# Attention's far exponentials: a square on VectorE and GpSimd in place of ScalarE, with key tiles in a mixed order

## The chip, the core and the metric

The kernel runs on one core of a Trainium2 chip. Times are microseconds of one execution on the device. The engines are TensorE (PE, its weight loads PEld), VectorE (DVE), ScalarE (ACT), GpSimd (POOL) and SyncE (SP), which issues most of the DMAs. Each works through its own queue in order, and semaphores order the queues among each other.

## The reference

Two sequences of 2048 tokens with 256 channels pass a layer norm, an attention with 16 heads of 16 channels, and a feed-forward part with shared and routed experts. What matters here is the attention (S = 2048):

```python
scores = jnp.einsum('bhqd,bhkd->bhqk', qh, k_rec) / math.sqrt(d)
t = jnp.arange(s, dtype=jnp.float32)
decay = jnp.exp(-LAMBDA_DECAY * jnp.abs(t[:, None] - t[None, :]))
scores = scores * decay[None, None, :, :]
attn = jax.nn.softmax(scores, axis=-1)
out = jnp.einsum('bhqk,bhkd->bhqd', attn, v_rec)
```

With LAMBDA_DECAY = 0.01, a score between tokens over 1024 rows apart is multiplied by less than exp(-10.24).

## The kernel before

It has three stages: a prologue (layer norm, values, first keys and queries), the attention, and the feed-forward part. The attention goes through 2 x 16 = 32 heads, numbered n = 2 it + par, in 16 pairs. `pairs` (line 505) writes the first and the last pair out and runs the others in two loops of one pair a round.

A head is 16 key tiles of 128 keys (step s), each against all 2048 queries in two halves of 1024. For each half PE makes scores into two banks of PSUM (`scores`, line 675). Three such pairs of banks take turns (`half_of`, line 482). The decay is put into keys and queries beforehand, so that only the tile's own block on the diagonal needs a correction: DVE multiplies it in PSUM with a mask (`mask`, line 591). ACT takes the exponential of the half, PSUM to SBUF (line 760), into one of three buffers of probabilities (`probs_of`, line 491). No maximum is subtracted, and the sums of the softmax come from a column of ones among the values. PE multiplies the probabilities with the values, four chunks of 512 queries side by side (`products`, line 685), and sums over the 16 tiles in a bank of its own for odd and one for even heads.

The queues are written out by hand:

- PE takes for step s: scores of half 0, products of step s - 2, scores of half 1 (lines 707 to 715); after step 4 the four transposes of the head in front (line 693), and in even heads of the first 12 pairs a projection for a later unit of heads after step 7 and one after step 11 (`project`, line 669).
- DVE takes the mask of each step, after step 2 a copy of the sums of the head in front (line 615), after step 5 their normalisation (line 619), and in even heads of the first 12 pairs three pieces after steps 8, 9 and 10 and three after steps 12, 13 and 14, which turn a projection into new keys or queries (`prepare`, lines 596 to 613, called in lines 646 to 649).
- ACT takes two exponentials a step.
- POOL copies the next head's values (line 562) when the products of the head in front are done, and in even heads of the first 12 pairs, before that, the weights of the next projection (line 565).
- SP stores prepared keys and queries and loads those of the next head (`load_halves`, line 146: 16 DMAs a head), from the time that the scores of the head in front are done.

Scores of a half wait until ACT has emptied the banks, three halves back. Both rings of three start anew with a head or a pair of heads, while 16 and 32 are no multiples of 3; so at the beginning of a head waits are for one half or one tile less far back:

```python
def halves_done(n, s, half):
    h = 2 * s + half
    return n * NHALF + (h - 1 if h < 2 else h - 2)
def tiles_done(par, n, s):
    return n * NSTEP + (s - 1 if par == 0 and s < 2 else s - 2)
```

ACT waits with `tiles_done` for the products that read the buffer of probabilities before (line 758).

Of the kernel before, what the change touches and what calls it, by code (L numbers as in the profile page):

```python
# [15 lines left out]
P = 128  # L16
# [415 lines left out]
def attention(nc, sem, ident, xT, V_all, decay, small, w_qk, w_unit, K_st, Q_st, work, ps, attn_dram, halves_dram, first_block, late_keys, **_):  # L432
# [17 lines left out]
    names = ("vg w proj_ps proj_free prep_link prep_sb sc_ps masked exp_done pv_done o_sb oT_ps rden_sb att_sb").split()  # L450
    s_ = {n: sem("a_" + n) for n in names}
    s_.update(att_out=sem("a_att_out"), stk0=sem("a_stk0"), stk1=sem("a_stk1"), out0=sem("a_out0"), out1=sem("a_out1"))
    bd_all, bd_link, flag = sem("a_bd_all"), sem("a_bd_link"), sem("a_flag")
# [28 lines left out]
    def half_of(s, half):  # L482

        return 2 * ((2 * s + half) % (ACC // 2))

    def halves_done(n, s, half):

        h = 2 * s + half
        return n * NHALF + (h - 1 if h < 2 else h - 2)

    def probs_of(par, s):

        return (par * NSTEP + s) % 3

    def tiles_done(par, n, s):

        return n * NSTEP + (s - 1 if par == 0 and s < 2 else s - 2)

    def own_block(s):

        at = s * P % HALF
        bank = half_of(s, s * P // HALF) + at // CH
        return ps[:, bank, at % CH:at % CH + P]

    def pairs(eng, pair):
        pair(0, True, True, False)
        with eng.Fori(1, NPAIR - PPU) as it:
            pair(it, True, False, False)
        with eng.Fori(NPAIR - PPU, NPAIR - 1) as it:
            pair(it, False, False, False)  # L510
        pair(NPAIR - 1, False, False, True)

    with nc.Block() as block:
        @block.sync
        def _(sp):
# [5 lines left out]
            def pair(it, prep, first, last):  # L521
# [35 lines left out]
        def _(pool):  # L557
            first_block["gpsimd_start"](pool)
            prime(pool, "vg", "w", "att_out", "stk0", "stk1", "out0", "out1")
# [9 lines left out]
            def pair(it, prep, first, last):  # L569
# [17 lines left out]
        def _(dve):  # L587
            first_block["vector_start"](dve)
            prime(dve, *"proj_free prep_link prep_sb masked o_sb rden_sb att_sb".split())

            def mask(n, s):

                wait(dve, "sc_ps", n * NHALF + 2 * s + s * P // HALF + 1)
                nc.vector.tensor_tensor(own_block(s), own_block(s), dmask, ALU.mult).then_inc(s_["masked"], 1)  # L594
# [41 lines left out]
            def pair(it, prep, first, last):  # L636
# [28 lines left out]
        def _(pe):  # L665
# [9 lines left out]
            def scores(par, n, s, half):  # L675
                wait(pe, "exp_done", halves_done(n, s, half))
                for q0, w, a in score_pieces(s, half):
# [3 lines left out]
                    m = nc.tensor.matmul(ps[:, half_of(s, half) + c % 2, q0 % CH:q0 % CH + w],  # L681
                                         K_st[tile, par, a, s * P:(s + 1) * P], Q_st[tile, par, a, at:at + w], start=True, stop=True)
                m.then_inc(s_["sc_ps"], 1)

            def products(par, n, s):

                wait(pe, "exp_done", n * NHALF + 2 * s + 2)
                for c in range(QC):
                    m = nc.tensor.matmul(ps[STRIP * c:STRIP * (c + 1), ACC + par], Vg[:, par, s], probs[:, probs_of(par, s), chunk(c)],  # L689
# [9 lines left out]
            def pair(it, prep, first, last):  # L699
                for par in range(2):  # L700
                    n = it * 2 + par
                    idle = ACC + 1 - par
# [1795 lines left out]
```

## Time and profile before

| what | us |
|---|---|
| runs, median of 3 (lowest, highest) | 1466.76 (1463.68, 1467.51) |
| span of the profiled execution (no other time of it is given) | 1469.9 |
| busy in it: PE, PEld | 1318.5, 587.3 |
| busy in it: ACT, DVE, POOL | 1145.2, 545.4, 214.7 |

The span runs from the first to the last instruction of one execution. Busy time of PE is that of matmuls, whose ends are modelled; PEld are weight loads beside them. In the rows further down, L760 is line 760 of the kernel, `ps` stands for PSUM, `work` for the large buffer in SBUF that holds probabilities, values and more.

### The profile page before, as it was taken

How to read it: one execution, taken by the hardware profiler on the slowest of the kernel's cores; microseconds unless marked ns; L12 is line 12 of the kernel's file. 1: busy time of each engine (PE TensorE's matmuls, PEld its weight loads, DVE VectorE, ACT ScalarE, POOL GpSimd, SP SyncE). 2: the span in 40 equal slices, each digit the busy share in tenths (PEclk: the TensorE clock that was granted, in tenths of full speed). 3: DMA queues.
4: the chain of work that ended last, by engine and by line, in shares of the span. 5: the costliest groups of instructions: out<-in, count | busy, mean ns of one | idle time of the engine just before them, and what ended most of it. 6: DMA issues, size and time to landing. Idle time of an engine off the chain costs nothing. (4 is left out here: it accounts for less than half of the span.)

```text
span 1469.9 us, 26673 instructions
## 1 busy us (share of the span) xinstructions
PE 1318.5 (90%) x8496; PEld 587.3 (40%) x8497; DVE 545.4 (37%) x1700; ACT 1145.2 (78%) x1419; POOL 214.7 (15%) x249
## 2 busy tenths in 40 slices
PE   7969999999999999999999999999987877879881
PEld 4623333333333333333333333333335655666641
DVE  4612323132232323323232222112223657674754
ACT  4559899998999999899999999999972444544531
POOL 2410000000000000000000000000002453333574
PEclk9979999999999999999999999999997997899996
DMA  7775566655466655556664555544973224457843
GB/s 190 233 181 146 127 153 153 133 143 120 117 158 138 156 111 143 121 139 155 139 152 93 143 121 127 111 93 100 239 150 85 82 95 154 149 183 215 266 131 101
DMA packets 141091, 210.96 MB, mean 144 GB/s; under 512 B 56864, under 2 KB 102816, under 8 KB 132768
## 3 DMA queue, kind: packets, MB, share of 16 engines
q1 hardware_dynamic: 134496, 192.86, 53.1%
q0 software_dynamic: 6144, 16.79, 3.6%
q8 instruction: 30, 0.49, 0.2%
q10 hardware_dynamic: 384, 0.52, 0.1%
q14 instruction: 37, 0.30, 0.1%
HBM read 147.19 MB, written 67.11 MB: 146 GB/s over the span
## 5 line engine op out<-in xcount | busy, mean ns | idle before, releaser
L760 ACT ACTIVATE work<-ps 128x1024 f32<-128x1024 f32 x1024 | 951.6, 1089 | 70.1 <-DVE ps L594 36.9
L689 PE MATMUL ps<-work 128*32 128x512 f32 x4096 | 548.5, 608 | 0.0
L681 PE MATMUL ps<-Q_st,K_st 64*128 64x512 f32 (+3 forms) x2432 | 440.9, 429 | 43.4 <-ACT work L760 28.3
L681 PEld LDWEIGHTS ps<-Q_st,K_st 64*128 64x128 f32 x2432 | 231.0, 184 | 541.9 <-ACT work L760 450.2
L594 DVE TENSOR_TENSOR ps<-ps,small 128x128 f32<-128x128 f32 x512 | 153.2, 299 | 728.9 <-PE ps L681 727.5
L562 POOL COPY work<-V_all 128x256 f32 (+1 forms) x32 | 12.8, 401 | 924.7 <-PE ps L689 924.0
L689 PEld LDWEIGHTS ps<-work 128*32 128x32 f32 x4096 | 80.9, 108 | 113.8 <-issue 87.8
L2120 POOL DMA_INDIRECT xs_dram<-part,decay x64 | 67.3, 1051 | 56.2 <-DVE decay L1888 24.0
L2138 POOL DMA_INDIRECT xT<-y_dram,decay x64 | 65.2, 1019 | 62.9 <-DMA xT<-y_dram,decay 31.2
L2297 PE MATMUL ps<-stack,work 128*128 x384 | 54.5, 288 | 0.2 <-issue 0.2
L2297 PEld LDWEIGHTS ps<-stack,work 128*128 128x128 f32 x384 | 50.2, 204 | 1.1 <-issue 1.1
L671 PE MATMUL ps<-xT,w_unit 128*128 (+1 forms) x96 | 47.6, 618 | 0.0
L2267 PE MATMUL ps<-decay,work 128*128 128x256 f32 x128 | 34.8, 427 | 11.7 <-DVE work L2346 11.7
L2204 ACT ACTIVATE work<-work,small 128x256 f32<-128x256 f32 x32 | 16.9, 590 | 35.1 <-POOL small L2146 35.0
L2353 DVE COPY work<-ps 128x512 f32<-128x512 f32 x48 | 33.0, 688 | 24.7 <-PE ps L2279 20.6
L2191 ACT COPY small<-stack 64x256 f32 x48 | 19.3, 402 | 29.1 <-PE ps L2316 24.2
L2279 PE MATMUL ps<-ident,work 128*128 128x128 f32 x192 | 32.4, 294 | 9.9 <-DVE work L2353 8.1
L2182 ACT ACTIVATE decay<-ps 128x128 f32<-128x128 f32 x48 | 13.2, 275 | 35.2 <-PE ps L2297 28.3
L2315 PE MATMUL ps<-stack,work 64*128 x96 | 34.9, 445 | 5.7 <-ACT work L2196 2.9
L2249 PE MATMUL ps<-xT,w_qk 128*128 128x512 f32 x64 | 32.7, 635 | 5.5 <-DVE work L2346 4.5
L1713 PE MATMUL ps<-w_qk,work 128*128 128x256 f32 x128 | 35.0, 433 | 2.7 <-ACT work L1747 2.7
L2196 ACT COPY work<-ps 128x512 f32<-128x512 f32 x48 | 28.1, 585 | 11.7 <-DMA y_dram<-work 5.4
(181 smaller groups left out, 1047.9 us busy)
## 6 DMA issues: line engine op xcount, KB each, us to landing
K_st<-halves_dram SPq DMA_DIRECT2D x248, 256.0 KB, 5.6
halves_dram<-work SPq DMA_DIRECT2D x64, 512.0 KB, 3.7
Q_st<-halves_dram SPq DMA_DIRECT2D x248, 128.0 KB, 5.6
work<-xs_dram SPq DMA_DIRECT2D x96, 128.0 KB
y_dram<-work SPq DMA_DIRECT2D x48, 256.0 KB
work<-in_L_attn_x SPq DMA_DIRECT2D x16, 512.0 KB, 4.8
attn_dram<-work SPq DMA_DIRECT2D x16, 256.0 KB, 6.6
work<-attn_dram SPq DMA_DIRECT2D x8, 512.0 KB
```

The source lines that it names most:

```text
L594: nc.vector.tensor_tensor(own_block(s), own_block(s), dmask, ALU.mult).then_inc(s_["masked"], 1)
L671: m = nc.tensor.matmul(ps[:, bank], w_unit[:, which, k], xT[:, k, at:at + CH] if isinstance(at, int) else xT[:, k, bass.ds(at, CH)], start ...
L681: m = nc.tensor.matmul(ps[:, half_of(s, half) + c % 2, q0 % CH:q0 % CH + w], K_st[tile, par, a, s * P:(s + 1) * P], Q_st[tile, par, a, at: ...
L689: m = nc.tensor.matmul(ps[STRIP * c:STRIP * (c + 1), ACC + par], Vg[:, par, s], probs[:, probs_of(par, s), chunk(c)], start=s == 0, stop=s ...
L760: nc.scalar.activation(probs[:, probs_of(par, s), half * HALF:(half + 1) * HALF], src, ACT.Exp, scale=SCALE).then_inc(s_["exp_done"], 1)
L1713: m = nc.tensor.matmul(bank[:, j * D:(j + 1) * D], aT[:, k, at:at + P], w_o[:, k], start=k == 0, stop=k == KD - 1)
L2120: nc.gpsimd.indirect_dma_start(xs_dram[r // 4], bass.IndirectOffsetOnAxis(ap=at, axis=0), xn[r % 2][:, j], None).then_inc(put_done[r % 2][ ...
L2138: nc.gpsimd.indirect_dma_start(yg[n % 2][:, j, i], None, y_dram[b], bass.IndirectOffsetOnAxis(ap=at, axis=0)).then_inc(fetched(n, j, i), 16)
L2267: m = nc.tensor.matmul(ps[:, down_banks(r)[half], j * D:(j + 1) * D], hid_s[:, h, at:at + P], w_ds[:, h], start=h == 0, stop=h == NSH - 1)
L2297: m = nc.tensor.matmul(ps[:, GU[g % 2], at:at + P], xsT[:, g % 2, k, a], w_gu[:, k * NE * P:(k + 1) * NE * P][:, bass.ds(experts[i][a], P) ...
L2315: nc.tensor.matmul(ps[:, DOWN[0], 0:D], hT[0:MR, g % 2], w_dr[0:MR, bass.ds(experts[i][0] * 2, D)], start=True, stop=True)
L2353: nc.vector.tensor_copy(xsT[:, g % 2].rearrange("p k a t -> p (k a t)"), ps[:, TR]).then_inc(tr_sb, 1)
```

## The change

The score of a key tile against a chunk of 512 queries, all of them over 1024 rows away, is so small that 1 + x + x²/2 stands for its exponential. There is one such chunk for the key tiles 0 to 3 (the last chunk) and 12 to 15 (the first chunk): 8 of 16 tiles, the far ones. For these DVE reads the chunk from PSUM and writes 1 + x, POOL squares it in place and then takes half of it plus a half. ACT does only the other chunk of that half, 512 columns in place of 1024. The half with the far chunk comes first in a far tile, that with the own block first in a near one. From the second head on, tiles come in an order in which near and far ones alternate. The very last head leaves all on ACT. PSUM banks and buffers of probabilities are numbered through all heads, for which the loop now takes three pairs a round: three rounds, then five pairs written out. POOL's copy of weights moves from the beginning of an even head to its step 2.

```diff
+    MIXED = [4, 0, 5, 1, 6, 2, 7, 3, 8, 12, 9, 13, 10, 14, 11, 15]
+    FAR_CHUNK = {kt: QC - 1 if kt < KT // 4 else 0 for kt in NATURAL if kt < KT // 4 or kt >= KT - KT // 4}
+    def half_of(turn, s, k):
+        return 2 * ((turn * NHALF + 2 * s + k) % (ACC // 2))
+    def halves_done(n, s, k):
+        return n * NHALF + 2 * s + k - 2
+    def probs_of(turn, s):
+        return (turn * NSTEP + s) % RING
+    def tiles_done(n, s):
+        return n * NSTEP + s - 2
     def pairs(eng, pair):
-        pair(0, True, True, False)
-        with eng.Fori(1, NPAIR - PPU) as it:
-            pair(it, True, False, False)
-        with eng.Fori(NPAIR - PPU, NPAIR - 1) as it:
-            pair(it, False, False, False)
-        pair(NPAIR - 1, False, False, True)
+        pair(0, True, True, False, 0)
+        with eng.Fori(1, 1 + 3 * RING, RING) as it:
+            for j in range(RING):
+                pair(it + j, True, False, False, (1 + j) % RING)
+        for it in range(1 + 3 * RING, NPAIR - 1):
+            pair(it, it < NPAIR - PPU, False, False, it % RING)
+        pair(NPAIR - 1, False, False, True, (NPAIR - 1) % RING)
...
+            def far_probs(turn, n, s, order):
+                kt = order[s]
+                if kt not in FAR_CHUNK:
+                    return
+                done = n * NFAR + far_before(order, s) + 1
+                p = probs[:, probs_of(turn, s), chunk(FAR_CHUNK[kt])]
+                wait(pool, "far_read", done)
+                nc.gpsimd.tensor_tensor(p, p, p, ALU.mult).then_inc(s_["far_sq"], 1)
+                wait(pool, "far_sq", done)
+                pool.sem_inc(far_link, 1)
+                nc.gpsimd.tensor_scalar(p, p, 0.5, 0.5, ALU.mult, ALU.add).then_inc(s_["far_sb"], 1)
...
-                    if par == 0 and prep:
-                        wait(pool, "proj_ps", 2 * it)
-                        weights((it // PPU + 1) % KD)
                     if not (last and par):
                         wait(pool, "pv_done", n * NSTEP)
                         values(n + 1, 1 - par)
+                        for s in range(NSTEP):
+                            if s == 2 and par == 0 and prep:
+                                wait(pool, "proj_ps", 2 * it)
+                                weights((it // PPU + 1) % KD)
+                            far_probs(turn, n, s, order)
...
+            def read_far(first, turn, n, s, kt):
+                c = FAR_CHUNK[kt]
+                wait(dve, "sc_ps", n * NHALF + 2 * s + 1)
+                if not (first and tiles_done(n, s) <= 0):
+                    wait(dve, "pv_done", tiles_done(n, s))
+                nc.vector.tensor_scalar(probs[:, probs_of(turn, s), chunk(c)], ps[:, half_of(turn, s, 0) + c % 2], SCALE, 1.0,
+                                        ALU.mult, ALU.add).then_inc(s_["far_read"], 1)
...
-                    for s in range(NSTEP):
-                        mask(n, s)
+                    for s, kt in enumerate(NATURAL if first and par == 0 else MIXED):
+                        if kt in FAR_CHUNK and not (last and par):
+                            read_far(first, 2 * third + par, n, s, kt)
+                        mask(2 * third + par, n, s, kt)
...
+            def scores(first, turn, n, s, k, order, far):
...
+                if not (first and halves_done(n, s, k) <= 0):
+                    wait(pe, "exp_done", halves_done(n, s, k))
+                if far or 2 * s + k < 3:
+                    far_read(first, n, s, k, order)
...
+            def products(turn, n, s, order, far):
...
                 wait(pe, "exp_done", n * NHALF + 2 * s + 2)
+                if far and kt in FAR_CHUNK:
+                    wait(pe, "far_sb", n * NFAR + far_before(order, s) + 1)
...
+                            chunks = [c for c in (2 * half, 2 * half + 1) if (last and par) or c != FAR_CHUNK.get(kt)]
+                            bank = half_of(turn, s, k) + chunks[0] % 2
+                            src = ps[:, bank:bank + len(chunks)].rearrange("p a b -> p (a b)")
+                            nc.scalar.activation(probs[:, probs_of(turn, s), chunks[0] * CH:(chunks[-1] + 1) * CH], src, ACT.Exp,
                                                  scale=SCALE).then_inc(s_["exp_done"], 1)
```

`far_read` on PE waits, three halves on, until DVE has read a far chunk.

## Rows read from the trace of the kernel before

**Rows 1.** Busy time by stage: stretch, us, PE, PEld, DVE, ACT, POOL, clock, DMA, GB/s.
```profile
86.20:1101.00 1014.80, 982.30 (x6774) 345.04 (x6774) 284.95 (x776) 956.24 (x1034) 21.60 (x46) 0.99 0.60 137
1101.00:1469.90 368.90, 275.77 (x1484) 197.70 (x1476) 219.25 (x797) 153.21 (x302) 161.22 (x167) 0.87 0.47 146
```

**Rows 2.** The same for heads 13, 14 (with projections) and 24.
```profile
500.96:531.30 30.34, 29.52 (x218) 10.29 (x212) 5.96 (x19) 29.58 (x32) 1.02 (x2) 1.00 0.58 133
531.30:564.37 33.07, 32.25 (x212) 11.27 (x216) 13.43 (x31) 29.91 (x33) 0.40 (x1) 1.00 0.60 139
848.34:877.83 29.49, 28.67 (x204) 10.01 (x208) 5.96 (x19) 29.48 (x33) 0.40 (x1) 1.00 0.55 111
```

**Rows 3.** Timeline of ACT in head 13: start, length, then what.
```profile
510.20 20.41 ACT L760 ACTIVATE work<-ps 128x1024 f32<-128x1024 f32 x22
```

**Rows 4.** Waits of the whole execution: us in total, times, longest.
```profile
ACT work L760 <- PE ps L689: 10.6, 15, 0.8
```

**Rows 5.** Timeline of PE in head 13.
```profile
507.22 1.07 PE L689 MATMUL ps<-work 128*32 128x512 f32 x8
...
508.65 0.66 PE L696 MATMUL ps<-ident,work 128*128 128x128 f32 x4
...
509.72 1.06 PE L689 MATMUL ps<-work 128*32 128x512 f32 x8
...
511.37 1.06 PE L689 MATMUL ps<-work 128*32 128x512 f32 x8
...
514.69 1.06 PE L689 MATMUL ps<-work 128*32 128x512 f32 x8
...
516.42 1.06 PE L689 MATMUL ps<-work 128*32 128x512 f32 x8
...
518.26 1.06 PE L689 MATMUL ps<-work 128*32 128x512 f32 x8
```

**Rows 6.** Timeline of PE in head 14, around the first projection.
```profile
544.21 0.50 PE L681 MATMUL ps<-Q_st,K_st 64*128 64x512 f32 x2
...
546.56 0.50 PE L681 MATMUL ps<-Q_st,K_st 64*128 64x512 f32 x2
546.98 1.07 PE L689 MATMUL ps<-work 128*32 128x512 f32 x8
547.98 0.50 PE L681 MATMUL ps<-Q_st,K_st 64*128 64x512 f32 x2
```

**Rows 7.** Timeline of ACT beside it: in brackets the idle time before.
```profile
547.09 1.02 ACT L760 ACTIVATE work<-ps 128x1024 f32<-128x1024 f32 x1 [0.98 <-PE ps L681]
548.85 6.52 ACT L760 ACTIVATE work<-ps 128x1024 f32<-128x1024 f32 x7 [0.74 <-DVE ps L594]
```

**Rows 8.** Groups of ACT by shape: busy us, mean ns, idle before.
```profile
L2169 ACT ACTIVATE work<-ps 128x512 f32<-128x512 f32 x16 | 9.5, 594 | 18.3 <-PE ps L2249 18.3
```

**Rows 9.** Timeline of DVE in head 14, after the first projection.
```profile
548.52 0.30 DVE L594 TENSOR_TENSOR ps<-ps,small 128x128 f32<-128x128 f32 x1 [4.89 <-PE ps L681]
...
550.44 0.68 DVE L607 TENSOR_REDUCE small<-ps 128x1 f32<-128x512 f32 x1
...
551.23 0.69 DVE L610 CAST work<-work 128x1024 fp32r<-128x1024 f32 x1
...
552.11 1.21 DVE L613 TENSOR_TENSOR work<-work 128x1024 fp32r<-128x1024 f32 x1
```

**Rows 10.** Groups of DVE by shape.
```profile
L617 DVE COPY work<-ps 128x512 f32<-128x512 f32 x32 | 21.8, 680 | 9.2 <-PE ps L689 9.2
```

**Rows 11.** Groups of POOL by shape.
```profile
L265 POOL TENSOR_TENSOR work<-work 128x1024 fp32r<-128x1024 f32 x8 | 18.8, 2354 | 27.3 <-DVE work L303 27.3
...
L565 POOL COPY w_unit<-w_qk 128x512 f32 x11 | 6.7, 614 | 1.4 <-issue 0.2
...
L271 POOL TENSOR_TENSOR small<-small 128x4 f32<-128x4 f32 x8 | 1.6, 199 | 0.6
```

**Rows 12.** SP's DMA issues in head 13: the last of the next head's loads.
```profile
511.55 0.53 SPq L157 DMA_DIRECT2D Q_st<-halves_dram  x1
```

More of the change, by code:

```diff
@@ L519, in store_att, with pair @@
                 sp.dma_start(dst[bass.ds(it // (H // 2), 1), bass.ds(it % (H // 2), 1)].rearrange("b u p t d -> p (b u t) d"), att).then_inc(s_["att_out"], 16)
-            def pair(it, prep, first, last):
+            def pair(it, prep, first, last, third):
                 for par in range(2):
@@ L567, in _, with pair @@
             values(0, 0)
-            def pair(it, prep, first, last):
+            def far_probs(turn, n, s, order):
[9 more added lines that the diff above has]
+                nc.gpsimd.tensor_scalar(p, p, 0.5, 0.5, ALU.mult, ALU.add).then_inc(s_["far_sb"], 1)
+            def pair(it, prep, first, last, third):
                 for par in range(2):
                     n = it * 2 + par
-                    if par == 0 and prep:
-                        wait(pool, "proj_ps", 2 * it)
-                        weights((it // PPU + 1) % KD)
+                    turn = 2 * third + par
+                    order = NATURAL if first and par == 0 else MIXED
                     if not (last and par):
@@ L634, in set_flag, with pair @@
                 nc.vector.tensor_scalar(flags[:, 0:1], bound_new[:, 0:1], SAFE, None, ALU.is_gt).then_inc(flag, 1)
-            def pair(it, prep, first, last):
+            def pair(it, prep, first, last, third):
                 for par in range(2):
@@ L673, in project, with far_read @@
                 m.then_inc(s_["proj_ps"], 1)
-            def scores(par, n, s, half):
-                wait(pe, "exp_done", halves_done(n, s, half))
-                for q0, w, a in score_pieces(s, half):
+            def far_read(first, n, s, k, order):
+                g = 2 * s + k - 3
+                if first and n == 0 and g < 0:
+                    return
+                before, at = (n, g // 2) if g >= 0 else (n - 1, NSTEP + g // 2)
+                tiles = order if g >= 0 else NATURAL if first and n == 1 else MIXED
+                if g % 2 == 0 and tiles[at] in FAR_CHUNK:
+                    wait(pe, "far_read", before * NFAR + far_before(tiles, at) + 1)
+            def scores(first, turn, n, s, k, order, far):
+                par = turn % 2
+                kt = order[s]
+                half = half_at(kt, k)
+                if not (first and halves_done(n, s, k) <= 0):
+                    wait(pe, "exp_done", halves_done(n, s, k))
+                if far or 2 * s + k < 3:
+                    far_read(first, n, s, k, order)
+                for q0, w, a in score_pieces(kt, half):
                     c = q0 // CH
@@ L697, in transposes, with pair @@
                 i.then_inc(s_["oT_ps"], 1)
-            def pair(it, prep, first, last):
+            def pair(it, prep, first, last, third):
                 for par in range(2):
                     n = it * 2 + par
+                    turn = 2 * third + par
                     idle = ACC + 1 - par
                     end = last and par
+                    order = NATURAL if first and par == 0 else MIXED
                     wait(pe, "vg", n + 1)
@@ L738, in _ @@
             for s in (NSTEP - 2, NSTEP - 1):
-                products(1, B * H - 1, s)
+                products((B * H - 1) % (2 * RING), B * H - 1, s, MIXED, False)
             first_block["router"](pe, 0, first_block["LG"])
```

76 lines of the change are left out of this document (40 added, 36 removed).

## The prediction

> **What bounds the kernel now.** I began with the stages: attention takes 1014.8 of the 1469.9 us of the profiled execution, and in it ACT is busy for 956 us and PE for 982 [rows 1]. Everything that the change touches lies there. The page has no separate time for this execution; its span lies 3.1 us over the median of the three runs shown (1466.76), so I sum differences and take them off that median.
>
> A busy PE says little, since ends of matmuls are modelled, so I looked next at single heads [rows 2]. Three lengths repeat: 30.34 us for an odd head, 33.07 for an even one with projections, 29.49 for an even one without. The 32 heads are 15 odd ones, 11 and 4 even ones of the two kinds, the first and the last. ACT in a stretch without stalls runs 22 exponentials in 20.41 us [rows 3]: less 1.1 for the last one, (20.41 - 1.1) / 21 = 0.92 us apart, or 1.84 for a tile of two, 29.4 for a head. That is the plain even head: **ACT bounds it**. The odd head has 0.9 more, at its end; 0.7 of it is ACT's wait for a product, 15 times, 10.6 us in all [rows 4]: the early wait of line 497.
>
> Then PE alone [rows 5]. After the transposes it has fallen behind, and from 509.72 to 514.69 its products come three tiles in 4.97 us, 1.66 each, with scores and products end to end; once it has caught up they come 1.84 apart (516.42, 518.26), at ACT's pace. So **PE needs 1.66 of ACT's 1.84 us**: it is the next limit, 10% behind. Of the 1.66, products take 1.00 (546.98 to 547.98 [rows 6]) and each half of scores 0.33. The transposes add 2.50 - 1.66 = 0.84. A projection puts the next scores 2.35 us behind those in front (544.21 to 546.56 [rows 6]) in place of 0.33, 2.0 more, and ACT stands still for much of it [rows 7].
>
> **The change, part by part.**
> *ACT gets less.* In 8 of 16 tiles one exponential has 512 columns in place of 1024. An ACTIVATE of 512 from PSUM lasts 0.594 us [rows 8], one of 1024 behind an idle stretch 1.02 [rows 7]: 0.43 less, so 0.49 apart. ACT then needs 24 x 0.92 + 8 x 0.49 = 26.0 us a head, 3.4 less. Over 30 heads this would be 103 us; it isn't to be had, for PE needs 16 x 1.66 + 0.84 = 27.4.
>
> *PE does as much as before*, with two waits more: for the read (before scores reuse its buffer) and for the scaled chunk (before far products). Both stand in front of everything PE has left, so ACT runs dry behind them when they are late; where they have been met, they cost nothing. But with three score buffers PE can't run at 1.66. For a near and a far tile: from the near tile's first scores to the far tile's second ones PE takes 1.66 + 0.33 + 1.00 = 2.99; scores to mask 0.54, mask to exponential 0.33 [rows 6, 9]; then ACT does that one and the next tile's first (0.92 each) and its second (1.02, and 0.04 to hand over, an estimate), whose buffer PE needs. That is 6.76 for two rounds, 3.38 a pair of tiles, against 3.32 for PE and 3.25 for ACT. A head: 8 x 3.38 + 0.84 = 27.9.
>
> *VectorE gets 8 reads a head.* A PSUM read of 512 columns takes 0.68 us [rows 10]; beside 16 masks that is 10 us of 28. The far tile's mask stands behind the read, but it needs the later scores anyway. It hides behind ACT and PE (uncovered, 0.68 each), except beside the projections: there a read and piece 1 (550.44 to 551.92, 1.48 us [rows 9]) stand in front of the third step's mask, and piece 2 (1.21) in front of the fourth step's read. By the order of lines 640 to 649 the mask starts some 0.8 us after PE and ACT could have used it, and the read 1.3 after it could; the second projection's read belongs to the last far tile, which no projection covers. I take 0.6 us for each projection (0 if slack takes it up, 1.3 if none does).
>
> *GpSimd gets two operations for each read.* The square has two inputs: 2.354 us for 1024 columns, 0.199 for 4 [rows 11], so 0.19 + 512 x 2.11 ns = 1.27. The scaling has one input and no row. Its bounds are the copy of 512 (0.614) and the two-input price (1.27) [rows 11]; I take 0.65, since the copy is nearest, with as many bytes in and out. With 0.08 between them (an estimate) a far tile takes GpSimd 2.0 of every 3.38 us. It must be in time too: scores 0.53 [rows 6, 7], read 0.68, hand-over 0.05, the 2.0, and 0.05 make 3.31 us after the far tile's first scores, and PE wants it at 3.38 + 0.33 = 3.71. There are 0.4 us to spare, and one far tile in a head hasn't got them: the copy of line 562 waits for the last products of the head in front and delays the first square by 0.65. That costs 0.25 a head. What such sums leave out (the odd head's last 0.2 now) I take as 0.25 too. An odd or plain head: 27.9 + 0.5 = 28.4; with projections 28.4 + 4.0 + 1.2 = 33.6.
>
> The subtraction of 1024 columns takes GpSimd 2.35 us and VectorE 1.21 [rows 9, 11]. The Trainium skill, "GPSIMD Engine Reference", section 4.1, sends elementwise work to VectorE for such a factor, about two with two inputs, and calls one-input work roughly line-rate. By its first half this change would lose wherever GpSimd ends last; the trace agrees with the factor, yet here the work fits beside PE, and by its second half the scaling is as cheap as I take it.
>
> *Order and numbering.* Near and far alternate, so GpSimd has two tiles' time for each. The first head keeps the natural order: four far tiles in a row at 2.0 against 1.84, twice, about +1.5. Buffers numbered through remove the early wait, which the 28.4 already holds. Three loop rounds of three pairs and straight code in place of one-pair loops: nothing, as head 1 runs outside a loop now and is as long as the other odd ones (the wait of line 497 comes in both). The weights' copy (0.614 [rows 11]) now stands behind one far tile: two tiles' time covers it. The next head's loads are issued by 512.1 in a head that ends at 531.3 [rows 12]; one of 28 us still covers them.
>
> *Sum.* Odd: 15 x (28.4 - 30.34) = -29. Even with projections: 11 x (33.6 - 33.07) = +6. Plain even: 4 x (28.4 - 29.49) = -4. First +1.5, last (all on ACT) 0. Together -26: **1441 us**.
>
> **The rivals.**
> (a) *PE at its bare pace*: nothing lost at the buffers, at GpSimd or beside the projections. Heads of 27.4 and 31.4: 15 x 2.94 + 11 x 1.67 + 4 x 2.09 = 71 less, 1396. For it: 1.66 was held for three tiles [rows 5]. Against: there ACT was ahead, which it won't be.
> (b) *Slower: the scaling costs what two inputs cost*, 1.27. Then the far chunk comes 3.93 us after its scores, and each of the eight pairs of tiles is 0.22 longer: 28.4 + 1.8 = 30.2, and 34.8 with projections, which hide some. -2 + 19 + 3, and 3 for the first head: +23, 1490. The point is a price of 1.05, where the 3.71 us are used up. Against it the copy's 0.614; for it that no row shows GpSimd with two steps of arithmetic.
> (c) *GpSimd and VectorE hold each other up.* No row shows a two-input operation of GpSimd beside VectorE's piece 1 or 2, which would now lie together. If whichever starts first makes the other wait, the cast of 0.69 or the subtraction of 1.21 [rows 9] waits for up to 1.27, or holds up a square, with a mask or a read behind it. At 1 us for each of 22 projections, 1463. The Trainium skill, "SBUF — State Buffer", section "Who interferes with whom", has such a lock for VectorE's two-input operations and for its copies in a two-port mode. No run here shows it.
> That the change doesn't take the columns off ACT has nothing for it.
>
> **How the numbers follow.** The forecast has 0.47, (a) 0.13, (b) 0.19, (c) 0.15; 0.06 is left for what I don't see, half of it slower. 0.3% is 4.4 us, about what a measurement of this kernel can tell from no change. Faster: 0.47, 0.13, a third of (c) and a little of the rest, 0.67. Same: most of (c), 0.11. Slower: (b) and half of the rest, 0.22. The forecast's own range is 1420 to 1460 (0 to 1.3 us a projection, up to 0.9 for the scaling). For 8 in 10 it takes in (c), the near part of (a) and what lies short of (b): 1410 to 1478.
>
> **What would show it.** Products 1.69 apart on PE in heads without projections; ACT busy under 27 us of 28.4; short exponentials near 0.49 apart; squares near 1.27 and scalings near 0.65 us; scores released by ACT, products seldom by GpSimd. A scaling over 1.05 us with products waiting for GpSimd proves me wrong by (b); longer casts or subtractions on VectorE point to (c); even heads at 31.4 to (a).

## The result, and the profile after

The changed kernel takes **1455.36 us** (median of 4 runs, 1452.27 to 1457.08) against 1465.22 us (1463.22 to 1467.51) for the kernel before on the same chip: ratio 0.9919, interval [0.9898, 0.9941]. It is faster by 9 to 15 us, where 26 were forecast. The profiled execution took 1457.08 us and spans 1453.1; before, the span was 1469.9. Of the 16.8 us between the spans 3.1 lie ahead of attention, where nothing was changed (over all the profiles that stretch takes 83.1 to 86.2 us), 13.4 in attention, and 0.3 behind it.

The stages (first two rows, as in [rows 1]) and single heads (as in [rows 2]): stretch, us, busy PE, PEld, DVE, ACT, POOL, clock, DMA share, GB/s. The heads are 11, 10 and 24, then 7, 8 and the last one; the last row is the beginning of head 8.

```profile
83.08:1084.45 1001.37, 971.47 (x6774) 340.50 (x6776) 451.81 (x1025) 870.96 (x1034) 432.44 (x543) 0.99 0.61 140
1084.45:1453.10 368.65, 277.44 (x1484) 198.72 (x1476) 219.15 (x797) 153.19 (x302) 160.82 (x167) 0.87 0.47 146
433.68:462.35 28.67, 28.48 (x214) 10.00 (x210) 11.32 (x27) 26.81 (x34) 14.01 (x18) 1.00 0.60 139
400.36:433.68 33.32, 32.26 (x216) 11.12 (x216) 18.82 (x39) 27.15 (x33) 13.78 (x19) 1.00 0.61 142
838.38:866.78 28.40, 28.38 (x212) 9.99 (x208) 11.34 (x27) 26.77 (x33) 13.63 (x17) 1.00 0.60 122
305.22:336.17 30.95, 28.08 (x208) 9.98 (x208) 11.33 (x27) 26.91 (x34) 14.04 (x18) 1.00 0.60 144
336.17:371.69 35.52, 34.28 (x224) 11.43 (x216) 18.82 (x39) 27.27 (x33) 13.76 (x18) 0.95 0.51 122
1037.18:1080.69 43.51, 35.50 (x230) 14.12 (x226) 11.97 (x46) 34.68 (x42) 2.76 (x5) 0.96 0.62 143
336.10:340.30 4.20, 4.20 (x24) 1.01 (x17) 0.73 (x2) 2.54 (x3) 0.07 (x1) 0.59 1.03 220
```

The three ordinary kinds of head are what was forecast: 28.67 (28.4 forecast), 33.32 (33.6) and 28.40 (28.4). In the plain one ACT is busy for 26.77 of 28.40 us and bounds it no longer; PE is busy for 28.38, as far as its modelled ends tell. The rows that stand out are heads 7 and 8 (13 and 14 are like them, 30.99 and 35.36) and the last head, 43.51 in place of 39.66. Summed over heads, in us:

| heads | before | after | difference | forecast |
|---|---|---|---|---|
| odd, without 7 and 13 (13) | 394.7 | 371.9 | -22.8 | -25 |
| with projections, without 8 and 14 (9) | 297.5 | 299.6 | +2.1 | +5 |
| plain even (4) | 118.0 | 113.6 | -4.4 | -4 |
| first | 34.3 | 36.1 | +1.9 | +1.5 |
| 7, 8, 13, 14 | 126.8 | 132.8 | +6.0 | -3 |
| last | 39.7 | 43.5 | +3.9 | 0 |

The whole shortfall is in the last two lines: 9 us in the four heads, 4 in the last.

Groups by shape, as in [rows 10 and 11]: the square, the scaling and the read.

```profile
L604 POOL TENSOR_TENSOR work<-work 128x512 f32<-128x512 f32 x248 | 257.9, 1040 | 413.5 <-DVE work L646 413.5
L607 POOL TENSOR_SCALAR work<-work 128x512 f32<-128x512 f32 x248 | 154.3, 622 | 49.1 <-POOL work L604 49.1
L646 DVE TENSOR_SCALAR work<-ps 128x512 f32<-128x512 f32 x248 | 171.2, 690 | 286.5 <-PE ps L752 286.1
```

VectorE's subtraction beside a projection takes 1.21 us, as before [rows 9], in every head but the first: in those heads GpSimd's scaling has ended 0.73 us before the subtraction begins. In the first head, whose tiles keep the natural order, the second subtraction and a square lie together, and the subtraction takes 2.08 us:

```profile
115.34 1.04 POOL L604 TENSOR_TENSOR work<-work 128x512 f32<-128x512 f32 x1 [0.21 <-DVE work L646]
...
115.38 2.08 DVE L666 TENSOR_TENSOR work<-work 128x1024 fp32r<-128x1024 f32 x1
```

Waits of the whole execution. The line of [rows 4], exponentials waiting for products, is gone; products wait little for the scaled chunk; weight loads for scores stand behind ACT (450.2 us before), and exponentials behind the mask. The third row is new: PE's scores waiting for "issue", twice, up to 2.7 us at a time. "Issue" stands where the profile names nothing that the engine waited for.

```profile
PEld ps L752 <- ACT work L841: 259.9, 307, 1.7
ACT work L841 <- DVE ps L638: 109.2, 157, 2.2
PE ps L752 <- issue: 5.4, 2, 2.7
PE ps L764 <- POOL work L607: 3.6, 13, 0.9
```

Timeline, three places: the end of head 7, PE in head 24 (compare [rows 5]), and PE in the last head.

```profile
332.10 0.50 PE L752 MATMUL ps<-Q_st,K_st 64*128 64x512 f32 x3
...
335.30 0.50 PE L752 MATMUL ps<-Q_st,K_st 64*128 64x512 f32 x2 [2.70 <-issue]
...
335.83 0.30 DVE L638 TENSOR_TENSOR ps<-ps,small 128x128 f32<-128x128 f32 x1 [2.89 <-PE ps L752]
336.17 1.02 ACT L841 ACTIVATE work<-ps 128x1024 f32<-128x1024 f32 x1 [2.17 <-DVE ps L638]
...
337.17 1.22 PE L752 MATMUL ps<-Q_st,K_st 64*128 64x512 f32 x4
...
850.13 1.07 PE L764 MATMUL ps<-work 128*32 128x512 f32 x8
...
863.99 1.06 PE L764 MATMUL ps<-work 128*32 128x512 f32 x8
...
1052.38 0.63 PE L1789 MATMUL ps<-ident,work 128*128 128x128 f32 x4 [1.79 <-issue]
```

From 332.60 to 335.30 PE does nothing, and the profile names no buffer, signal or transfer that releases it. The queues of VectorE and ACT take up nothing for 2.8 and 2.9 us (from 332.79 and 333.10), though ACT still works on an exponential until 334.01. That is where the first round of the loop of line 533 ends: in all three queues the last record is the loop's branch. The second round ends at 523 us with the same picture. Behind it the granted clock is 0.59 for 4.2 us (last row of the heads' fence), its lower level of 1.2 GHz for most of them, and four matmuls of scores take 1.22 us together that take 0.73 elsewhere. In the last head PE stands for 1.79 us. Its queue is at line 1778, which waits for the loads of the next stage's constants, and the last of these lands at 1052.29. Again the lower level follows.

### The profile page after: what moved, and what is told of

It is laid out like the page before. It is cut to its first block and busy times, and to the rows that moved or that the text cites. A ratio compares the mean times of both kernels' runs of the same rounds, so it can differ in the third digit from the quotient of the medians.

```text
span 1453.1 us, 27412 instructions
## 1 busy us (share of the span) xinstructions
PE 1307.9 (90%) x8496; PEld 582.6 (40%) x8497; DVE 711.9 (49%) x1948; ACT 1059.6 (73%) x1419; POOL 624.5 (43%) x745
## 5 line engine op out<-in xcount | busy, mean ns | idle before, releaser
L841 ACT ACTIVATE work<-ps 128x1024 f32<-128x1024 f32 (+1 forms) x1024 | 866.0, 928 | 139.4 <-DVE ps L638 109.2
L752 PE MATMUL ps<-Q_st,K_st 64*128 64x512 f32 (+3 forms) x2432 | 422.8, 423 | 33.6 <-ACT work L841 14.3
L604 POOL TENSOR_TENSOR work<-work 128x512 f32<-128x512 f32 x248 | 257.9, 1040 | 413.5 <-DVE work L646 413.5
L752 PEld LDWEIGHTS ps<-Q_st,K_st 64*128 64x128 f32 x2432 | 225.0, 185 | 515.8 <-ACT work L841 259.9
L646 DVE TENSOR_SCALAR work<-ps 128x512 f32<-128x512 f32 x248 | 171.2, 690 | 286.5 <-PE ps L752 286.1
L607 POOL TENSOR_SCALAR work<-work 128x512 f32<-128x512 f32 x248 | 154.3, 622 | 49.1 <-POOL work L604 49.1
L2285 ACT ACTIVATE work<-work,small 128x256 f32<-128x256 f32 x32 | 16.9, 590 | 34.4 <-POOL small L2227 34.3
L2263 ACT ACTIVATE decay<-ps 128x128 f32<-128x128 f32 x48 | 13.2, 276 | 36.2 <-PE ps L2378 36.1
```

Source lines behind the costliest of these rows:

```text
L604: nc.gpsimd.tensor_tensor(p, p, p, ALU.mult).then_inc(s_["far_sq"], 1)
L607: nc.gpsimd.tensor_scalar(p, p, 0.5, 0.5, ALU.mult, ALU.add).then_inc(s_["far_sb"], 1)
L646: nc.vector.tensor_scalar(probs[:, probs_of(turn, s), chunk(c)], ps[:, half_of(turn, s, 0) + c % 2], SCALE, 1.0, ALU.mult, ALU.add).then_i ...
L752: m = nc.tensor.matmul(ps[:, half_of(turn, s, k) + c % 2, q0 % CH:q0 % CH + w], K_st[tile, par, a, kt * P:(kt + 1) * P], Q_st[tile, par, a ...
L841: nc.scalar.activation(probs[:, probs_of(turn, s), chunks[0] * CH:(chunks[-1] + 1) * CH], src, ACT.Exp, scale=SCALE).then_inc(s_["exp_done ...
```

## The experiments

Times are medians; each ratio is to the kernel before, run beside it on the same chip. That kernel took 1465.22 to 1470.53 us there, so between experiments ratios and heads are compared more safely than times. The experiments put three questions: what the loop costs, what the last head waits for, and what the two parts of the change are worth.

**The loop written out.**

```diff
-        with eng.Fori(1, 1 + 3 * RING, RING) as it:
-            for j in range(RING):
-                pair(it + j, True, False, False, (1 + j) % RING)
-        for it in range(1 + 3 * RING, NPAIR - 1):
+        for it in range(1, NPAIR - 1):
```

> The changed kernel with its fourteen middle pairs of heads written out in place of three loop rounds of three pairs; nothing else differs. Theory: the two ends of loop rounds cost it 8 to 9 us (in the trace 2.9 us without an instruction on PE, ACT and DVE, and 3.4 us of half TensorE clock behind it, over heads 7, 8, 13 and 14). Then heads 7 and 13 come to 28.7 us (30.95 and 30.99 in the changed kernel), heads 8 and 14 to 33.2 (35.52, 35.36), and the time falls from 1455 to about 1446. Rival: what stretches these four heads sits at their loads or projections and only happens to fall at the end of a round; then the four heads keep their lengths and the time stays within 2 us of 1455.

1439.4 us, ratio 0.9805 [0.9777, 0.9832]. Heads 7, 8 and the last:

```profile
305.19:333.87 28.68, 28.59 (x212) 9.98 (x208) 11.34 (x27) 26.81 (x33) 14.09 (x18) 1.00 0.59 136
333.87:367.03 33.16, 32.18 (x220) 11.23 (x216) 18.47 (x39) 27.17 (x34) 13.80 (x18) 1.00 0.62 146
1027.23:1067.68 40.45, 33.99 (x230) 13.80 (x226) 11.87 (x46) 34.38 (x42) 2.76 (x5) 1.00 0.63 154
```

The four heads lose 9.1 us, as the theory said, and the clock stays at 1.00. The time fell by more, 16 us between the two medians: the last head is 3.1 shorter, since the constants happened to come almost in time there (PE waited 0.22 us), and nine heads with projections lost 0.13 each. That makes 13.4 us of attention; the other 2 to 3 are not explained. Against the kernel before, attention is now 26.8 us shorter.

**The long round in the kernel before.**

```diff
-        with eng.Fori(1, NPAIR - PPU) as it:
-            pair(it, True, False, False)
-        with eng.Fori(NPAIR - PPU, NPAIR - 1) as it:
-            pair(it, False, False, False)
+        with eng.Fori(1, 10, 3) as it:
+            for j in range(3):
+                pair(it + j, True, False, False)
+        for it in range(10, NPAIR - 1):
+            pair(it, it < NPAIR - PPU, False, False)
```

> The kernel before with its loop in the changed kernel's shape: three rounds of three pairs and the rest written out; order, numbering and exponentials are those of before. Theory: a round of three pairs costs 2.9 us without an instruction at each of its two ends, whatever the pairs do, and half clock behind it; the heads at these places grow by 4 us together at each end, and the time goes up by 6 to 9 us over the kernel before (1465 to about 1472). Rival: the gap comes from the changed pairs themselves (their waits on both sides of the end); then heads 7, 8, 13 and 14 keep 30.3 and 33.1 us and the time stays within 2 us.

1475.84 us, ratio 1.0067 [1.0044, 1.0089]: 9.8 us slower, a little over the theory's 6 to 9. Heads 7, 8, 13 and 14 grew by 2.7, 1.0, 2.3 and 1.3. The timeline at the first end of a round:

```profile
336.15 0.50 PE L682 MATMUL ps<-Q_st,K_st 64*128 64x512 f32 x3
...
339.71 0.50 PE L682 MATMUL ps<-Q_st,K_st 64*128 64x512 f32 x2 [3.05 <-issue]
...
341.75 1.02 ACT L761 ACTIVATE work<-ps 128x1024 f32<-128x1024 f32 x1 [3.41 <-PE ps L690]
```

Nothing of the change is in this kernel but the shape of its loop, and the stop is there. VectorE went on after 0.3 us this time, which led to the next run.

**Rounds of two pairs.**

```diff
-        with eng.Fori(1, NPAIR - PPU) as it:
-            pair(it, True, False, False)
-        with eng.Fori(NPAIR - PPU, NPAIR - 1) as it:
-            pair(it, False, False, False)
+        with eng.Fori(1, 11, 2) as it:
+            for j in range(2):
+                pair(it + j, True, False, False)
+        for it in range(11, NPAIR - 1):
+            pair(it, it < NPAIR - PPU, False, False)
```

> The kernel before with five loop rounds of two pairs (the rest written out). Rows so far: at the end of a round an engine stands for 2 to 3 us where its round has 422 (VectorE), 482 (ACT) or over 1500 (PE) instructions, and for 0.4 at most where it has 313 (SP), 278 (VectorE), 221 (GpSimd) or 162 (ACT, one pair); PE's 502 of one pair cost 0.1 to 0.3. Theory: what counts is the length of the engine's own round; with two pairs PE has some 1000 and stands for 2.5 to 3 us, VectorE (186) under 0.4, and ACT (322) lies between the rows; four ends inside the loop, at 3.5 us each as in the run with rounds of three, make it 12 to 16 us slower than the kernel before. Rival: the standing comes with what a round of three pairs does (registers, addresses), and two pairs cost under 1 us an end: within 4 us of the kernel before.

1483.2 us, ratio 1.0111 [1.0081, 1.0141]: 14 us slower, within the theory's 12 to 16. ACT (322 instructions a round) went on within 0.3 us and VectorE (186) within 0.4; PE stopped at each of the four ends. PE's waits for issue, from 120 to 1030 us, and its timeline at the second end:

```profile
PE ps L682 <- issue: 12.2, 4, 3.4
...
406.16 0.79 PE L682 MATMUL ps<-Q_st,K_st 64*128 64x512 f32 x2 [3.20 <-issue]
```

So it is each engine's own round that counts. The counts of PE leave out matmuls, of which there are as many as weight loads; with them its rounds have 926 instructions for one pair (no stop), 1850 for two and over 2700 for three (both 2.7 to 3.4 us by the rows here). ACT's limit lies between 322 and 482, VectorE's between 278 and 422. On PE's queue the record of the branch itself lasts 3.3 to 3.8 us at these ends, but 0.2 us at the ends of one pair in the kernel before and 0.1 at the last end of a loop, where nothing is repeated.

What the engines stand for can be seen among the transfers, of which the profile has a kind called "instruction" (queue, packets, MB, share of the DMA engines). Four stretches: the kernel before from 205 to 820 us, with ten ends of rounds of one pair; then one stop each, of the changed kernel (332.6 to 335.3), of the kernel before with rounds of three (336.6 to 339.7) and with rounds of two (402.0 to 406.2):

```profile
q1 hardware_dynamic: 46071, 83.33, 58.1%
...
q8 instruction: 1, 0.02, 2.2%
q14 instruction: 2, 0.02, 1.9%
...
q8 instruction: 1, 0.02, 2.0%
q14 instruction: 1, 0.01, 1.0%
...
q8 instruction: 1, 0.02, 1.8%
```

Through ten short rounds not one instruction is loaded. Each stop of PE, in all eight ends of long rounds, has one load on q8, which begins 0.9 to 1.5 us after PE's branch and takes 0.9 to 1.3. On q14 there are as many loads as other engines stop: two (ACT and VectorE), one (ACT), none. So at the jump back these engines wait for instructions. Which queue serves which engine is concluded from these counts, and why PE stands for 1.7 us and more after its load has ended is not explained. In the written-out kernel 57 such loads fall between 205 and 820 us, and from 84 to 1030 us PE has no wait for issue at all: loading alone stops nothing, the jump back does.

**The constants one head earlier.** In the changed kernel:

```diff
+                    if last and not par:
+                        wait(sp, "att_out", 16 * H // 2)
...
+                        first_block["sync"](sp)
                     if par == 0 and not first:
                         store_att(it - 1)
                     if end:
-                        wait(sp, "att_out", 16 * H // 2)
...
-                        first_block["sync"](sp)
```

> The changed kernel, loop as it is, but the loads of the next stage's constants are issued one head earlier on SP: behind the loads of head 31, in front of the store of pair 14, in place of behind that store. Theory: in the changed kernel the last head is 43.5 us long because PE waits 1.79 us for these constants at its first router transposes and runs at half clock for 3.4 us behind that; with the constants there in time it comes to 40.4 us (its length in the written-out kernel, where the wait was 0.22), 3 us less, and the time from 1455 to about 1452. Rival: the last head is long because the order of its tiles puts the masks and the router's work badly together; then it stays at 43 to 44 us.

The loads now stand ahead of pair 14's store on SP, where they stood behind it. 1453.85 us, ratio 0.9908 [0.9875, 0.994], and the last head is 45.30 us long, not 40.4. By itself this fits the rival, but a timeline of DVE in that head shows a fault of the edit:

```profile
1051.12 0.42 DVE L680 TENSOR_TENSOR work<-ps,small 128x256 f32<-128x256 f32 x1 [2.93 <-DMA attn_dram<-work]
```

Two of the constants' issues took 15.2 us together, and the store had to wait for them; the normalisation waited for that store, and masks and scores behind it. One wait had been put in the place of another.

**The constants two heads earlier**, ahead of no store that is waited for:

```diff
                         load_halves(sp, K_st, Q_st, halves_dram, n + 1, 1 - par, s_[f"stk{1 - par}"])
+                    if isinstance(it, int) and it == NPAIR - 2 and par:
+                        wait(sp, "att_out", 16 * H // 2)
...
+                        first_block["sync"](sp)
```

> The changed kernel, loop as it is, with the constants' loads of the next stage issued on SP behind the loads of head 30, two heads earlier than in the changed kernel and ahead of no store that is waited for: when they were issued one head earlier they stood in front of pair 14's store, and VectorE waited 2.9 us for that store. Theory: the last head is long because the constants are late, so that it comes to 40.2 to 40.5 us (43.5 in the changed kernel), and the time falls by 3 us to about 1452. Rival: the last head of this kernel is long for another reason, as the one-head experiment could be read: then it stays over 42.

1451.94 us, ratio 0.9886 [0.9859, 0.9913]. The last head:

```profile
1039.77:1080.05 40.28, 34.22 (x230) 13.81 (x226) 11.85 (x46) 34.35 (x42) 2.75 (x5) 0.98 0.46 93
```

The theory's length; the time alone couldn't tell 3 us apart. Late constants make 3.2 of the 3.9 us, the remaining 0.6 is not explained.

**The numbering alone**, written out:

```diff
-    MIXED = [4, 0, 5, 1, 6, 2, 7, 3, 8, 12, 9, 13, 10, 14, 11, 15]
-    FAR_CHUNK = {kt: QC - 1 if kt < KT // 4 else 0 for kt in NATURAL if kt < KT // 4 or kt >= KT - KT // 4}
+    MIXED = NATURAL
+    FAR_CHUNK = {}
-        return FAR_CHUNK[kt] // 2 if kt in FAR_CHUNK else kt * P // HALF
+        return 0
```

> The changed kernel written out, natural order of the tiles, no far chunks: all sixteen tiles of a head go to the exponentials on ACT as before, so that only the numbering of the buffers is left of the change. Theory: it takes away the wait at the end of the odd heads, which come to 29.5 us like the plain even ones (30.34 before); 15 heads by 0.85 are 13 us: about 1452. The far chunks with their order are then worth what is left, about 6 us against the written-out kernel with them (1446). Rival: the wait at the end of odd heads only moves to another place, heads stay at 30.3 and the time at 1465; then all of the gain is the far chunks'.

1449.78 us, ratio 0.9889 [0.9867, 0.9911]: 16 us off, a little more than the 13 expected. Heads with projections, odd, plain:

```profile
521.38:554.49 33.11, 33.11 (x222) 11.52 (x218) 13.27 (x31) 29.97 (x33) 0.96 (x2) 1.00 0.61 142
554.49:583.68 29.19, 29.19 (x208) 10.10 (x208) 5.96 (x19) 29.19 (x33) 0.40 (x1) 1.00 0.58 137
862.25:891.62 29.37, 29.37 (x212) 10.18 (x208) 5.96 (x19) 29.37 (x34) 0.40 (x1) 1.00 0.51 109
```

ACT is busy for all of 29.19 and 29.37 us. The far chunks, with all that VectorE and GpSimd do for them, take off the 10 us that are left to 1439.4: 0.5 us of an odd head, 1.0 of a plain one, nothing of one with projections, and the first head is 2 us longer.

**GpSimd's arithmetic left out**, in the changed kernel:

```diff
-                nc.gpsimd.tensor_tensor(p, p, p, ALU.mult).then_inc(s_["far_sq"], 1)
-                wait(pool, "far_sq", done)
-                pool.sem_inc(far_link, 1)
-                nc.gpsimd.tensor_scalar(p, p, 0.5, 0.5, ALU.mult, ALU.add).then_inc(s_["far_sb"], 1)
+                pool.sem_inc(s_["far_sb"], 1)
```

> The changed kernel without GpSimd's square and scaling (GpSimd only passes the signal on, so that far probabilities are left as VectorE's 1 + x). Theory: GpSimd is in time nearly everywhere; odd and plain heads fall by 0.25 us at most from 28.6 and 28.4, which is the price taken for the one far tile of a head that hasn't got the time, and the heads with projections by no more than 0.5: 3 to 9 us in all. Rival: GpSimd's arithmetic (or a lock with VectorE) is what keeps the heads at 28.4 in place of PE's bare pace of 27.4; then heads fall by about 1 us each, and with projections by 2, some 40 us.

1441.07 us, ratio 0.9824 [0.9796, 0.9852]. Heads 10, 11 and 24:

```profile
397.65:430.46 32.81, 32.19 (x216) 11.09 (x216) 18.41 (x39) 27.16 (x34) 1.02 (x2) 1.00 0.62 145
430.46:459.01 28.55, 28.55 (x214) 10.06 (x210) 11.39 (x27) 26.80 (x34) 0.40 (x1) 1.00 0.60 139
833.22:861.60 28.38, 28.38 (x212) 9.99 (x208) 11.41 (x27) 26.77 (x34) 0.40 (x1) 1.00 0.60 122
```

By heads the theory holds: 0.1 us of an odd head, nothing of a plain one, 0.5 of one with projections, and 1.3 of the first. Attention is 9.3 us shorter, 2.4 of them in the last head, where GpSimd had no such work: PE's wait for the constants there was 0.85 us in place of 1.79. The time fell by 14, more than either account of the heads gives; the rest is not explained.

**Natural order with the far chunks**, written out; only `MIXED = NATURAL`.

> The written-out kernel with its far chunks made on VectorE and GpSimd, but with the tiles of every head in natural order: four far tiles in a row at either end of a head, in place of near and far in turn. Theory: GpSimd takes 1.04 + 0.20 + 0.62 = 1.86 us for a far tile, more than PE's 1.66, and has one tile's time for it in place of two: odd and plain heads 29.5 to 30.5 us, those with projections 34 to 36.5, and a time of 1475 to 1505, over the kernel before. Rival: GpSimd's queue is long enough ahead that the order does not matter: heads within 0.3 us of the alternating ones, and about 1439.

1531.71 us, ratio 1.0445 [1.0416, 1.0474]. The direction is the theory's, the size beyond its 1475 to 1505: plain heads 30.56, but odd ones up to 32.1 and those with projections 36.65; attention is 87 us longer than in the written-out kernel. By the profile's names products waited 25.7 us for GpSimd (0.3 in the same stretch of the written-out kernel), and 52.0 us, once a head, for ACT. These waits, and the second kind at the beginning of a head without projections:

```profile
ACT work L838 <- DVE ps L635: 169.2, 232, 3.1
PE ps L761 <- ACT work L838: 52.0, 30, 1.7
PE ps L761 <- POOL work L604: 25.7, 45, 0.9
...
937.58 0.62 POOL L604 TENSOR_SCALAR work<-work 128x512 f32<-128x512 f32 x1 [0.20 <-POOL work L601]
...
938.34 1.06 PE L761 MATMUL ps<-work 128*32 128x512 f32 x8 [1.73 <-ACT work L838]
```

That kind is GpSimd's too: all 30 of these waits end 0.15 us after one of its scalings, while the exponentials of that tile had been done for 2 us. GpSimd copies the next head's values only when the last products of the head in front are done, so its first square of a head comes late, and in a row of far tiles it can't catch up: the next products come 1.82 us apart, where PE alone needs 1.66. Exponentials wait longer for masks as well (86.8 us in the written-out kernel), and in 12 of the 24 projections a subtraction and a square lay together and the subtraction took 2.08 us. The order also puts the near tiles in a row, which ACT bounds; what that costs by itself no run shows.

**No masks**, written out; the masks' operation on VectorE is left out, and ACT waits for the scores.

> The written-out kernel without VectorE's masks: the exponentials wait for the scores alone (the multiplication of the diagonal blocks by the decay mask is left out). Theory: what holds a head at 28.4 to 28.7 us over PE's bare 27.4 is the round trip through three score buffers, in which the mask stands between scores and exponential; without it the loop is about 0.3 us shorter than the 3.38 reckoned for a pair of tiles and PE's own 3.32 decide: plain heads 27.4 to 27.7 (28.4 now), odd ones 27.4 to 27.8 (28.7), those with projections about 32.1 (33.2). Rival: PE's matmuls themselves take longer than the 1.66 us of a tile when ACT is never ahead; then the heads stay within 0.3 us of 28.4 and 28.7.

1417.2 us in one run. Heads with projections, odd, plain:

```profile
510.54:542.51 31.97, 31.89 (x220) 10.88 (x216) 15.30 (x23) 27.16 (x33) 13.40 (x18) 1.00 0.62 140
542.51:570.95 28.44, 27.76 (x212) 9.46 (x208) 6.91 (x11) 26.70 (x34) 14.43 (x19) 1.00 0.62 149
840.46:868.26 27.80, 27.72 (x212) 9.45 (x208) 6.91 (x11) 26.72 (x34) 13.63 (x18) 1.00 0.52 115
```

Between the two: plain heads lose 0.6 us, a little short of the theory, those with projections 1.2, as it said, odd ones only 0.24, within the rival's bound. The mask is a limit in plain heads, by its place between scores and exponential or by VectorE's time for it, which this run doesn't separate; what holds the odd ones is open.

**VectorE's pieces in four steps**, written out:

```diff
                     nc.vector.tensor_tensor(bound[:, which:which + 1], bound[:, which:which + 1], bound_new[:, which:which + 1], ALU.max)
+                elif piece == 2:
                     nc.vector.tensor_copy(pt[:, :, 0].bitcast(F32R), split).then_inc(s_["prep_link"], 1)
-                elif piece == 2:
+                elif piece == 3:
-                        if prep and par == 0 and s >= 8 and s < 11:
+                        if prep and par == 0 and s >= 8 and s < 12:
-                        if prep and par == 0 and s >= 12 and s < 15:
+                        if prep and par == 0 and s >= 12 and s < 16:
```

> The written-out kernel with VectorE's work on a projection spread over four steps in place of three: the reduction and the running bound in the second, the cast in the third, the subtraction in the fourth. Theory: the second piece (1.48 us), which stands in front of the third step's mask, costs a projection about 0.4 us and the subtraction less; heads with projections fall from 33.16 to 32.3 to 32.8, eleven times, and the time from 1439 to about 1433. Rival: VectorE is early enough there and the projection's own matmuls on PE are all of the 4.5 us that these heads are longer; then they stay at 33.1.

**1429.53 us**, ratio 0.9743 [0.9709, 0.9777]: the lowest of the kernels that leave nothing out. A head with projections and the odd one behind it:

```profile
513.73:546.39 32.66, 32.46 (x222) 11.36 (x220) 18.56 (x39) 27.31 (x34) 15.45 (x18) 1.00 0.61 137
546.39:574.67 28.28, 28.28 (x208) 9.74 (x208) 11.35 (x27) 26.73 (x32) 13.86 (x18) 1.00 0.62 150
```

0.5 us less for the one, as expected, and 0.4 for the other, which was not. The subtraction now lies beside GpSimd's scaling, which takes 1.36 us in place of 0.62, 22 times; here the subtraction runs from 292.13 to 293.35:

```profile
292.47 1.36 POOL L604 TENSOR_SCALAR work<-work 128x512 f32<-128x512 f32 x1 [0.20 <-POOL work L601]
```

**This with the earlier constants**, at both places.

> Written out, constants one head earlier, and VectorE's pieces in four steps together. Theory: the parts add up, since they lie in different heads: 1439 less 6 for the pieces, and for the constants between 0 and 1 (the written-out kernel waited only 0.22 us for them): about 1433, under both kernels. Rival: the earlier constants' transfers hold up the keys and queries of head 31 or shorter heads uncover a transfer; then it is no better than the written-out kernel with the pieces in four steps.

> Written out, VectorE's pieces in four steps, and the constants' loads behind those of head 30. Theory: heads as in the run with the pieces in four (28.3 odd, 32.7 with projections, 28.4 plain) and a last head of 40.2 in place of 41.2: about 1428.5 against 1429.5, at any rate not slower. Rival: the constants' transfers in head 29 delay the loads of head 31, and head 31 starts late: slower than 1429.5 by 2 us or more.

One head earlier: 1434.09 us, 0.9771 [0.9735, 0.9807], last head 43.87: pair 14's store again, so the parts did not add up. Two heads earlier: 1432.71 us, 0.9756 [0.9735, 0.9778], last head 40.51 but head 30 0.7 longer. Neither can be told from the kernel without the earlier constants.

## Why the prediction was right or wrong

- **The bound and the sum by heads: right, in part by luck.** ACT's 29.4 us no longer bound a head: 28.67, 33.32 and 28.40 came, against 28.4, 33.6 and 28.4. Once the loop is out of the way, attention is 26.8 us shorter where the sum said 26, and the time is 1439.4 where it said 1441. But its parts are off and cancel: odd heads lost 26 us in all where 29 were forecast, those with projections grew by 1 in place of 6. Within a head too: from 850.13 to 863.99 eight products are 1.73 apart, where 1.69 was forecast, and a plain head has nothing of the 0.25 for GpSimd.
- **The loop: the step that failed.** "Three loop rounds of three pairs and straight code in place of one-pair loops: nothing, as head 1 runs outside a loop now". Head 1 could show that a round of one pair costs nothing (no engine stood over 0.33 us at its end), but not what a round of three costs. In the changed kernel three engines stand for 2.7 to 2.9 us at each end, and with the lower clock behind it an end costs 4.6 us, 9.1 for the two. That is shown from both sides: taken away by writing the loop out, added to the kernel before by its long round. What the engines stand for are loads of instructions at the jump back, seen among the transfers of all eight such ends. A rule of the Trainium skill, "Runtime: NRT & Kernel Launch", section "Instruction fetch mechanics", bears on it: an engine's memory holds 512 instructions, PE's 2048, and a taken branch to a place outside the current window of two pages must wait until that is fetched. The runs agree in kind, PE going on at 926 instructions where ACT stops at 482. By 512 and 2048 alone ACT, VectorE (422) and PE at 1850 would have had room for a whole round; they stop all the same, and the measurement decides.
- **The last head: failed too.** "last (all on ACT) 0" looked at its work and not at what it waits for. From the issue of the first of its loads to the landing of the last constant 32.1 us pass (31.3 before, 30.5 written out); PE asks for them 29.4 us after that issue (31.7 before, 29.4 written out), as the two heads over which they are loaded became shorter. The late constants cost 3.2 us, by the run with the constants two heads earlier.
- **GpSimd: right in effect, the square mis-sized.** 1.04 us where 1.27 was forecast, from a row of two different inputs; the scaling 0.62 where 0.65 was. Rival (b) had its point at 1.05 for the scaling and falls. The quarter of a us a head that was taken for GpSimd's lateness is 0.1 in odd heads, nothing in plain ones. That the order is needed is shown: natural order loses 92 us to the written-out kernel.
- **Rival (c): the lock is there, and the changed kernel misses it by luck.** The prediction knew no run that shows it and feared that VectorE's pieces and GpSimd's operations "would now lie together". In the changed kernel the subtraction lies beside none of them, in every head but the first: it begins 0.73 us after a scaling's end, a distance that no sum foresaw. Where they lie together, one holds up the other: the subtraction takes 2.08 us beside a square in place of 1.21, the scaling 1.36 beside a subtraction in place of 0.62. The cast kept its 0.68 in all these runs. Even so the kernel with 22 such scalings has the lowest time. **Rival (a)**: heads of 27.4 were not reached even without masks.
- **The projections**: 5.2 us over a plain head were forecast, 4.0 for PE and 1.2 for VectorE's pieces; 4.9 came. Splitting the pieces gave back 0.5, and 0.4 of the next head. GpSimd's arithmetic holds 0.5 of such a head, where the sum had the 0.25 of every head. How the rest is divided no run shows.

## What to carry to other kernels

When a change makes a loop's round longer, count the instructions of each engine's round and price the ends of rounds, with the clock behind them; in the rows the signs are a wait for "issue" of some us at the branch and a load of instructions in it. When heads or stages become shorter, look at every transfer whose cover was their length. And an operation taken off the bounding engine is worth only the distance to the next one: a plain head freed ACT of 2.6 us (29.37 to 26.77) and became 1.0 shorter, and over all heads 10 us came back.

## What the runs showed that was not expected

- A stop of 2.7 to 3.4 us of PE at the end of a round of 1850 instructions or more, none at 926; of ACT at 482 and VectorE at 422, none at 322 or fewer. In each stop instructions are loaded, and after each stop of PE the granted clock was at the 1.2 GHz level for 3.4 us or more.
- VectorE's subtraction of two inputs in SBUF and GpSimd's square or scaling hold each other up when they lie together: 2.08 us in place of 1.21, 1.36 in place of 0.62.
- GpSimd's square of a chunk with itself, 128 x 512, takes 1.04 us; its scaling with two steps of arithmetic takes 0.62, as long as a copy of that size [rows 11].
- An issue on SP can be what takes time: two DMAs into `w_unit` held SP for 12 to 15 us, and what stands behind them in its queue waits.
